# A Perceiver megakernel on one core: a smaller first piece of the context, the first local keys ahead of the query projection, and a new order table

## The chip, the cores and the metric

The kernel runs on one core of a Trainium2 chip. The metric is the device time in microseconds (us) of one execution. TensorE is called PE, its weight loads PEld, VectorE DVE, ScalarE ACT, GpSimd POOL and SyncE SP. Everything is float32; a float32 matmul shows in the trace as two records, so "x4" in a row of the trace is two matmuls.

## The reference, cut to what matters

Two layers of three residual stages each work on 16 batches of 32 tokens with 128 features; the context has 512 rows for each batch. Each stage adds to x what it computes from a layer norm of x.

```python
x = x + L0_xattn(layernorm(x), ctx)   # queries Wq, keys Wk; query i sees keys 16i..16i+15 only ("local")
x = x + L0_attn(layernorm(x))         # RWKV: a scan over the tokens
x = x + L0_ffn(layernorm(x))          # 8 experts, the top 2 of them, and a shared one
x = x + L1_xattn(layernorm(x), ctx, ctx, mask)   # all 512 keys, a mask, softmax
x = x + L1_attn(layernorm(x))         # linear attention and a feed-forward part
x = x + L1_ffn(layernorm(x))          # 16 experts, top 1, a capacity of 32 tokens
```

The keys and values of `L1_xattn` depend on the context alone, so they can be computed at any time after the context is there.

## The kernel before, in words

All 512 tokens fit into one tile of 128 x 512, and so do the 512 keys of one batch. The context stands in SBUF as `ctx`, transposed, 512 columns for each batch. It is loaded by SP in five pieces, given by `PIECES` (line 281): batches 0-1, 2-3, 4-7, 8-11, 12-15. `context(c)` (line 334) issues piece c with its own semaphore `ctx_in{c}`, and `piece_of(b)` says which of them batch b waits for. SP issues, in this order: x, `early` (the first weights), pieces 0, 1, 2, `next`, the first half of the context with tokens in rows (`ctok`), piece 3, `late` (all other weights), piece 4, the second half of `ctok`, and then, behind waits, masks and the weights of the last stage.

The batches go through the middle of the network in two halves (h = 0 and 1) of eight. The work is cut into streams, one generator each, and each `yield` ends a turn:

- `local()` (letter L) is `L0_xattn`. On PE: seven matmuls on zeros (line 1277) from the start on; four transposes of the normalised x (line 1227, called from `turn_lnT`), which wait for DVE's normalised tokens (line 690); the projection of the queries (line 1283), which waits for ACT's copy of those transposes to SBUF (line 487); then for each batch c one matmul with `wk0`, the local keys (line 1306), into bank 0 or 1 in turn. DVE scales the queries (line 722) and multiplies each batch's keys with them (line 732, `prod`); key c + 2 waits for product c, because both use one bank. Then come head sums (line 1294), a softmax, its transposes (line 1315), `z` = probabilities times context (line 1328, with copies by ACT at line 517) and the output (line 1337).
- `projections()` (P) are the keys (line 1266) and values (line 1270) of `L1_xattn`, written to banks 3 and 4 in turn; ACT (lines 498, 500) or DVE (773, 775) copies each out.
- `small_stages(h)` (a, b) are `L0_attn` and `L0_ffn` of half h. On ACT the first of it is exp(w) (line 528), which waits for `late`; DVE's line 784 waits for that. The hidden layer's last product is at line 1411; its silu is at ACT's lines 570 and 571, with a load of the activation table ahead.
- `scores()` (S, line 1438), `exponentials()` (S on ACT, 583), `least()` (S on DVE, 964), `turns()` (T, transposes of the probabilities, line 1452, with copies out of the bank by ACT, 594, or DVE, 975) and `outputs()` (V, 1469) are `L1_xattn`.
- `linear_stages(h)` (c, d) is `L1_attn` and the gate of `L1_ffn`; its transposes are at lines 1558 and 1227, its hidden layer at 1571 and 1584, the counts of the experts at 1609 and 1613, the dispatch at 1626.
- e, h, i, y, o are the last stage: 1643, 1653, 1665, 1677.
- G on PE is `keep_busy` (line 1694): each turn one 128 x 128 matmul into a bank that nothing reads. It puts something on PE where it would wait.

What sets the order on each engine is the table `TURNS` (line 68). It is written out: "L P L8" is a turn of L, a turn of P, eight turns of L. `run` (line 311) goes through it; a letter whose stream is at its end does nothing. Each engine runs its instructions strictly in this order, and waits on semaphores where the data aren't there.

Of the kernel before, what the change touches and what calls it, by code (L numbers as in the profile page):

```python
# [11 lines left out]
P = 128  # L12
BATCH, SEQ, D = 16, 32, 128
TOK = BATCH * SEQ
TT = TOK // P
KEYS = 512
# [5 lines left out]
HB, HT, HTOK = BATCH // 2, TT // 2, TOK // 2  # L22
# [30 lines left out]
def columns(pack):  # L53

    at, out = 0, {}
    for name, n in pack:
# [10 lines left out]

TURNS = {
# [7 lines left out]
    "DVE": (  # L76
# [7 lines left out]
    "ACT": (  # L84
# [4 lines left out]
    "POOL": (  # L89
        "L a L a4 b a3 b L a3 b2 a b4 a b a b3 L c3 d c d L a c d2 a c L b2 d c L c b2 d3 a c b d2 c ")}  # L90

# [26 lines left out]
def program(nc, x_d, early_d, next_d, late_d, ctx_d, ctok_d, mask_d, w1_d, w2_d, moeb_d, out_d):  # L118
    with ExitStack() as stack:
# [5 lines left out]
        def sig(name):  # L125
            if name not in sems:
                sems[name] = stack.enter_context(nc.semaphore(name))
            return sems[name]
# [15 lines left out]
        ctx = sb("ctx", CTX)  # L144
# [133 lines left out]
        mr = [small[:, 64 * i:64 * (i + 1)] for i in range(8)]  # L278
        m4 = [small[:, 516 + 4 * i:520 + 4 * i] for i in range(9)]

        PIECES = (0, 2, 4, 8, 12, BATCH)

        def piece_of(b):

            return sum(1 for p in PIECES[1:-1] if b >= p)

# [44 lines left out]
        def _(sp):  # L331
            def context(c):
                k = slice(KEYS * PIECES[c], KEYS * PIECES[c + 1])
                sp.dma_start(ctx[:, k], ctx_d[:, k]).then_inc(sig(f"ctx_in{c}"), 16)
# [3 lines left out]
            context(0)  # L338
            context(1)
            context(2)  # L340
            sp.dma_start(following[:, :], next_d).then_inc(sig("next_in"), 16)
            sp.dma_start(ctok[0], ctok_d[:, 0:CTX // 2]).then_inc(sig("ctok_in0"), 16)
            context(3)
            sp.dma_start(late[:, :], late_d).then_inc(sig("late_in"), 16)
            context(4)
            sp.dma_start(ctok[1], ctok_d[:, CTX // 2:CTX]).then_inc(sig("ctok_in1"), 16)

            sp.wait_ge(sig("z_ps"), HB)
# [869 lines left out]
        def _(pe):  # L1218
# [24 lines left out]
            def wait_norm(h):  # L1243
                pe.wait_ge(sig(f"lnT_ready{h}"), turned[h])
# [29 lines left out]
            def local():  # L1274
# [4 lines left out]
                pe.wait_ge(sig("early_in"), 16)  # L1279
                turn_lnT(0, X[0], range(TT))  # L1280
                yield
                wait_norm(0)
                mm(Y[0][:, :], wt("wq0"), lnT[:, :], start=True, stop=True).then_inc(sig("q0_ps"), 1)
                yield
                for h in range(2):
# [11 lines left out]
                            last.then_inc(sig("s0_ps"), 1)  # L1297

                    for c in range(HB * h, HB * (h + 1)):
                        if c in PIECES:  # L1300
                            pe.wait_ge(sig(f"ctx_in{piece_of(c)}"), 16)
                        if c % HB >= 2:
                            pe.wait_ge(sig("prod_ready"), c - 1)
                        elif h:
                            pe.wait_ge(sig("z_out"), HB)
                        mm(bank[c % 2][:, :], wt("wk0"), ctx[:, KEYS * c:KEYS * (c + 1)], start=True, stop=True).then_inc(sig("k0_ps"), 1)  # L1306
                        yield
                        if c % 4 == 3 and c % HB > 4:
                            for k in range(c - 7, c + 1):
                                headsum(k)  # L1310
                                if k % 4 == 3:
                                    yield
# [486 lines left out]
```

## Time and profile before

| | us |
|---|---|
| median of 3 runs | 236.79 |
| lowest, highest | 235.16, 237.21 |
| the profiled execution | 235.32 |
| its span, first to last instruction | 233.4 |
| PE busy / DVE / ACT / POOL | 218.7 / 178.0 / 131.7 / 34.5 |
| mean granted clock of PE | 0.993 |

The profiled execution's own time is 1.9 us over its span, and 1.5 us below the median. The share of busy time is a mean over stages with different limits. PE counts as busy from the start of a matmul to its modelled end, so a busy PE isn't PE at its peak. The chain of waits goes back from the last instruction, at each step to what released it. A landing time is counted from the issue of the transfer to its semaphore.

### The profile page before, as it was taken

The numbers are of one execution on the slowest core, as the hardware profiler recorded it, in microseconds if no ns is written. First come the engines' busy times: TensorE is split into PE (matmuls) and PEld (weight loads), VectorE is DVE, ScalarE is ACT, GpSimd is POOL, SyncE is SP. The second block draws the span as 40 slices with busy tenths as digits, with TensorE's granted clock in tenths as the row PEclk, the third lists the DMA queues.
The fourth block names the chain that finished last, engine by engine and source line by source line (L and its number), as shares of the span: only waits on it lengthen the run. The fifth ranks groups of instructions, "written<-read, shape, count | busy, mean of one in ns | idle before, by whom it ended". The sixth has DMA issues, their size and how long they took to land.

```text
span 233.4 us, 5227 instructions
## 1 busy us (share of the span) xinstructions
PE 218.7 (94%) x1992; PEld 156.2 (67%) x1992; DVE 178.0 (76%) x514; ACT 131.7 (56%) x292; POOL 34.5 (15%) x55
## 2 busy tenths in 40 slices
PE   7699999999999999879989998999999989898995
PEld 6332595747786796546656776768577768797495
DVE  2176743999955669999788979999998958646672
ACT  2201473445368327689999987988887741030330
POOL 2120000022205123602040230020001031201000
PEclk9999999999999889999999999999999999999999
DMA  6999959700000000006100340000005998500001
GB/s 204 412 421 448 420 219 213 150 0 0 1 3 0 0 3 0 1 3 159 24 0 0 95 91 3 3 0 4 0 3 177 449 442 386 219 0 0 3 3 45
DMA packets 2905, 26.88 MB, mean 115 GB/s; under 512 B 448, under 2 KB 704, under 8 KB 1344
## 3 DMA queue, kind: packets, MB, share of 16 engines
q1 hardware_dynamic: 2880, 26.54, 31.3%
q8 instruction: 16, 0.26, 0.4%
q14 instruction: 9, 0.07, 0.1%
HBM read 26.28 MB, written 0.26 MB: 114 GB/s over the span
## 4 chain that ended last, share of the span: by engine, by line
PE 72%; DVE 15%; ACT 6%; issue 3%; DMA 3%; SPq 0%; POOL 0%; DVEq 0%
PE bank L1452 8%; PE bank L1328 6%; PE bank L1306 6%; PE bank L1438 6%; PE bank L1266 5%; PE bank L1469 4%; DVE ctx_sb L964 4%; PE bank L1270 3%; DMA ctx_sb<-ctx 3%; PE bank L1411 2%; PE bank L1694 2%; ACT ctx_sb L583 2%; PE bank L1249 2%; PE bank L1394 2%; PE bank L1584 2%
## 5 line engine op out<-in xcount | busy, mean ns | idle before, releaser
L583 ACT ACTIVATE ctx_sb<-ctx_sb,small_sb 128x512 f32<-128x512 f32 x64 | 45.8, 720 | 3.1 <-DVE small_sb L964 3.1
L964 DVE CUSTOM_DVE_ANT_0 ctx_sb<-bank,mask_sb 128x512 f32<-128x512 f32 x64 | 42.2, 683 | 1.7 <-PE bank L1438 1.5
L1452 PE MATMUL bank<-early_sb,ctx_sb 128*128 128x128 f32 x256 | 36.3, 278 | 3.1 <-DVE work_sb L975 2.7
L1452 PEld LDWEIGHTS bank<-early_sb,ctx_sb 128*128 128x128 f32 x256 | 27.9, 141 | 14.6 <-issue 7.9
L385 POOL TENSOR_TENSOR rstd_sb<-veps_sb,minus_half_sb 128x2 f32<-128x2 f32 (+1 forms) x15 | 11.0, 733 | 128.8 <-DVE veps_sb L684 128.8
L594 ACT COPY work_sb<-bank 128x512 f32<-128x512 f32 x40 | 22.9, 579 | 7.7 <-PE bank L1452 7.0
L1438 PE MATMUL bank<-k_sb,work_sb 32*128 32x512 f32 x128 | 18.5, 638 | 1.7 <-DVE small_sb L964 1.1
L1266 PE MATMUL bank<-ctx_sb,early_sb 128*128 128x512 f32 x32 | 16.3, 610 | 1.8 <-DMA ctx_sb<-ctx 1.8
L732 DVE SCALAR_TENSOR_TENSOR work_sb<-bank,early_sb,work_sb 128x512 f32<-128x512 f32 x16 | 11.8, 747 | 8.2 <-PE bank L1306 7.7
L1469 PE MATMUL bank<-work_sb,v_sb 128*32 128x128 f32 x512 | 17.3, 276 | 0.4 <-ACT work_sb L594 0.4
L1270 PEld LDWEIGHTS bank<-late_sb,ctx_sb 128*128 128x128 f32 x128 | 15.4, 191 | 2.8 <-issue 2.6
L1469 PEld LDWEIGHTS bank<-work_sb,v_sb 128*32 128x32 f32 x512 | 13.1, 109 | 5.7 <-ACT work_sb L594 3.5
L975 DVE COPY work_sb<-bank 128x512 f32<-128x512 f32 x24 | 16.4, 682 | 0.5 <-PE bank L1452 0.2
L1270 PE MATMUL bank<-late_sb,ctx_sb 128*128 128x128 f32 x128 | 16.2, 277 | 0.0
L1306 PE MATMUL bank<-ctx_sb,early_sb 128*128 128x512 f32 x32 | 15.8, 605 | 0.2 <-DVE work_sb L732 0.2
L498 ACT ACTIVATE k_sb<-bank,early_sb 128x512 f32<-128x512 f32 x12 | 8.0, 686 | 12.9 <-PE bank L1266 12.9
L517 ACT COPY work_sb<-bank 128x512 f32<-128x512 f32 x16 | 9.2, 583 | 8.3 <-PE bank L1328 8.2
L583 ACT ACTIVATION_READ_ACCUMULATOR ctx_sb<-ctx_sb,small_sb 128x1 f32 x64 | 12.4, 193 | 0.0
L325 DVE TENSOR_TENSOR work_sb<-bank,early_sb 128x512 f32<-128x512 f32 x16 | 10.2, 676 | 0.9 <-PE bank L1315 0.7
L500 ACT COPY v_sb<-bank 128x512 f32<-128x512 f32 x12 | 7.0, 582 | 5.0 <-PE bank L1270 5.0
L1306 PEld LDWEIGHTS bank<-ctx_sb,early_sb 128*128 128x128 f32 x32 | 5.2, 189 | 6.6 <-issue 3.2
L487 ACT ACTIVATE lnT_sb<-bank 128x256 f32<-128x256 f32 (+1 forms) x7 | 2.9, 415 | 11.8 <-PE bank L1227 7.7
(262 smaller groups left out, 403.4 us busy)
## 6 DMA issues: line engine op xcount, KB each, us to landing
k_sb<-moe_w SPq DMA_DIRECT2D x1, 4096.0 KB, 12.8
ctx_sb<-moe_w SPq DMA_DIRECT2D x1, 4096.0 KB, 17.2
ctx_sb<-ctx SPq DMA_DIRECT2D x3, 1024.0 KB, 15.4
late_sb<-late SPq DMA_DIRECT2D x1, 2966.5 KB, 21.7
mask_sb<-ctx_tok SPq DMA_DIRECT2D x1, 2048.0 KB, 14.3
v_sb<-ctx_tok SPq DMA_DIRECT2D x1, 2048.0 KB, 27.8
mask_sb<-mask SPq DMA_DIRECT2D x4, 512.0 KB, 7.9
mask_sb<-mask SPq DMA_DIRECT2D x8, 256.0 KB, 4.5
```

What stands on the lines that cost most here:

```text
L583: s.activation(sc[u % NSC], sc[u % NSC], ACT.Exp, bias=smin[:, u:u + 1], scale=-1.0, accum_out=rsum[:, u:u + 1]).then_inc(sig("p1_ready"), 1)
L594: s.copy(pt[j % NPT], bank[TB[j % 2]][:, :]).then_inc(sig("pT_act"), 1)
L732: v.scalar_tensor_tensor(prod[c % HB].rearrange("p (q j) -> p q j", j=LOCAL), bank[c % 2][:, :].rearrange("p (q j) -> p q j", j=LOCAL), wt ...
L964: v.tensor_tensor_reduce(sc[u % NSC], bank[SB[u % GROUPS]][:, :], mask[:, KEYS * b:KEYS * (b + 1)], MASK_BIG, 3e38, ALU.add, ALU.min, smin ...
L975: v.tensor_copy(pt[j % NPT], bank[TB[j % 2]][:, :]).then_inc(sig("pT_dve"), 1)
L1266: last = mm(dst[:, :], wt("wk1"), ctx[:, KEYS * b:KEYS * (b + 1)], start=True, stop=True)
L1270: last = mm(dst[:, P * k:P * (k + 1)], ctx[:, at:at + P], wt("wv1"), start=True, stop=True)
L1306: mm(bank[c % 2][:, :], wt("wk0"), ctx[:, KEYS * c:KEYS * (c + 1)], start=True, stop=True).then_inc(sig("k0_ps"), 1)
L1328: last = mm(bank[c % 2][:, P * k:P * (k + 1)], ctok[h][:, at:at + P], mix[c % NE][:, P * k:P * (k + 1)], start=True, stop=True)
L1438: mm(bank[SB[g]][:, :], qc[b][r, :], k1[r, KEYS * b:KEYS * (b + 1)], start=True, stop=True)\
L1452: last = nc.tensor.transpose(bank[TB[u % 2]][:, P * k:P * (k + 1)], sc[u % NSC][:, P * k:P * (k + 1)], wt("ident"))
L1469: last = mm((bank[OB2][r, 0:P] if b == BATCH - 1 else bank[OB1][r, at:at + P]), vkey[:, b, k, r], pt[(GROUPS * b + g) % NPT][:, P * k:P * ...
```

## The change

`PIECES` gets a further cut: batch 0 is now a piece of its own (256 KB) and batch 1 another, so the context comes in six pieces, and SP issues one more transfer ahead of the rest. On PE the local keys of batch 0 stand ahead of the projection of the queries. And all four rows of `TURNS` are new. Nothing is computed in another way, and no matmul is added or removed but for `keep_busy`: 32 turns of it are reached before, 24 now.

```diff
-        PIECES = (0, 2, 4, 8, 12, BATCH)
+        PIECES = (0, 1, 2, 4, 8, 12, BATCH)
...
             context(2)
+            context(3)
             sp.dma_start(following[:, :], next_d).then_inc(sig("next_in"), 16)
             sp.dma_start(ctok[0], ctok_d[:, 0:CTX // 2]).then_inc(sig("ctok_in0"), 16)
-            context(3)
+            context(4)
             sp.dma_start(late[:, :], late_d).then_inc(sig("late_in"), 16)
-            context(4)
+            context(5)
             sp.dma_start(ctok[1], ctok_d[:, CTX // 2:CTX]).then_inc(sig("ctok_in1"), 16)
...
                 turn_lnT(0, X[0], range(TT))
                 yield
+                def keys(c):
+                    mm(bank[c % 2][:, :], wt("wk0"), ctx[:, KEYS * c:KEYS * (c + 1)], start=True, stop=True).then_inc(sig("k0_ps"), 1)
+                pe.wait_ge(sig("ctx_in0"), 16)
+                keys(0)
+                yield
                 wait_norm(0)
                 mm(Y[0][:, :], wt("wq0"), lnT[:, :], start=True, stop=True).then_inc(sig("q0_ps"), 1)
...
                     for c in range(HB * h, HB * (h + 1)):
-                        if c in PIECES:
-                            pe.wait_ge(sig(f"ctx_in{piece_of(c)}"), 16)
-                        if c % HB >= 2:
-                            pe.wait_ge(sig("prod_ready"), c - 1)
-                        elif h:
-                            pe.wait_ge(sig("z_out"), HB)
-                        mm(bank[c % 2][:, :], wt("wk0"), ctx[:, KEYS * c:KEYS * (c + 1)], start=True, stop=True).then_inc(sig("k0_ps"), 1)
-                        yield
+                        if c:
+                            if c in PIECES:
+                                pe.wait_ge(sig(f"ctx_in{piece_of(c)}"), 16)
+                            if c % HB >= 2:
+                                pe.wait_ge(sig("prod_ready"), c - 1)
+                            elif h:
+                                pe.wait_ge(sig("z_out"), HB)
+                            keys(c)
+                            yield
...
     "PE": (
-        "L P L P L11 P4 L P L8 P L2 a L2 P L a P L a3 P L P L4 P6 a P L P2 L3 a L2 a2 L P L P L a L a P a2 b "
+        "L P L3 P L9 P4 L P L8 P L2 a L P L2 a P L a3 L P L2 P L2 P6 L P a P L P L3 a L a2 L2 P L a L a L P L "
```

Lines of the new file are 1 to 2 higher than before's up to line 1277, the local keys are at line 1287 in place of 1306, and lines from 1294 on are 10 or 11 higher. The order of the instructions is shown at three places.

**PE, the first matmuls.** Before:

```order
L1277 MATMUL bank<-work_sb 128x256 x7
L1266 MATMUL bank<-ctx_sb,early_sb 128x512
L1227 MATMUL bank<-early_sb,xn_tok_sb 128x128 x4
L1266 MATMUL bank<-ctx_sb,early_sb 128x512
L1283 MATMUL bank<-lnT_sb,early_sb 128x512
L1306 MATMUL bank<-ctx_sb,early_sb 128x512 x8
```

Now:

```order
L1279 MATMUL bank<-work_sb 128x256 x7
L1268 MATMUL bank<-ctx_sb,early_sb 128x512
L1229 MATMUL bank<-early_sb,xn_tok_sb 128x128 x4
L1287 MATMUL bank<-ctx_sb,early_sb 128x512
L1293 MATMUL bank<-lnT_sb,early_sb 128x512
L1268 MATMUL bank<-ctx_sb,early_sb 128x512
L1287 MATMUL bank<-ctx_sb,early_sb 128x512 x7
```

The local keys of batch 0 have taken the place of the second key projection, which now stands behind the queries' projection. Behind these rows PE's order is unchanged up to the start of the second half's local keys. On ACT the copy of the first projection (line 498, now 500) now stands ahead of the copy of the transposed x (487, now 489).

**PE, the linear attention of the second half, some 35 us before the end.** The names: `mask_sb` holds that stage's tiles, `small_sb` the gate's; line 1694 (now 1705) is `keep_busy`. Before:

```order
L1552 MATMUL bank5<-mask_sb 32x128 x8
L1694 MATMUL bank2<-early_sb 128x128 x3
L1558 MATMUL bank5<-early_sb,mask_sb 128x128 x2
L1694 MATMUL bank2<-early_sb 128x128 x3
L1249 MATMUL bank1<-late_sb,mask_sb 128x128 x2
L1694 MATMUL bank2<-early_sb 128x128 x9
L1227 MATMUL bank5<-early_sb,xn_tok_sb 128x128 x2
L1694 MATMUL bank2<-early_sb 128x128 x2
L1609 MATMUL bank7<-small_sb,late_sb 128x32
L1613 MATMUL bank7<-small_sb,late_sb 128x16
L1571 MATMUL bank6<-lnT_sb,late_sb 128x256 x2
```

Now:

```order
L1563 MATMUL bank5<-mask_sb 32x128 x8
L1569 MATMUL bank5<-early_sb,mask_sb 128x128 x2
L1251 MATMUL bank1<-late_sb,mask_sb 128x128 x2
L1620 MATMUL bank7<-small_sb,late_sb 128x32
L1624 MATMUL bank7<-small_sb,late_sb 128x16
L1705 MATMUL bank2<-early_sb 128x128 x7
L1229 MATMUL bank5<-early_sb,xn_tok_sb 128x128 x2
L1705 MATMUL bank2<-early_sb 128x128 x2
L1582 MATMUL bank6<-lnT_sb,late_sb 128x256 x2
```

Six of `keep_busy` around line 1558 and two of the nine behind it are gone, and the counts of the experts (1609, 1613) have moved from behind the transposes to ahead of the keep-busy work. Further on, the seven of `keep_busy` ahead of the last dispatch (line 1626) are four now, and four stand earlier in place of one.

**ACT, the hidden layer of the second half's experts (line 570 is the silu), at some 120 us.** Before:

```order
L556 ACTIVATE mask_sb<-bank,late_sb 128x256
L594 COPY work_sb<-bank 128x512
L556 ACTIVATE mask_sb<-bank,late_sb 128x256
L570 ACT_TABLE_LOAD
L570 ACTIVATE mask_sb<-mask_sb 128x1024
L571 ACTIVATE mask_sb<-mask_sb 64x256
L583 ACT_TABLE_LOAD
```

Now:

```order
L558 ACTIVATE mask_sb<-bank,late_sb 128x256 x2
L572 ACT_TABLE_LOAD
L572 ACTIVATE mask_sb<-mask_sb 128x1024
L573 ACTIVATE mask_sb<-mask_sb 64x256
L596 COPY work_sb<-bank 128x512
L585 ACT_TABLE_LOAD
```

A copy that empties one of the two banks of the transposed probabilities (line 594, now 596) has moved from ahead of the silu to behind it. In that middle part (the second half's small stages beside `L1_xattn`) many turns of S, T and V have changed places by one or two on all engines.

## Rows read from the trace of the kernel before

**Rows 1.** The chain of waits, first 11 us: start us, us, what.

```profile
1.64 6.57 DMA ctx_sb<-ctx
8.25 1.12 PE bank L1266 x2
9.38 0.44 PE bank L1227 x4
9.82 0.86 PE bank L1266 x2
10.68 1.04 PE bank L1283 x2
```

**Rows 2.** Instructions in order of time, first 13 us: start us, us, engine, line, what.

```profile
1.31 5.13 PE L1277 MATMUL bank<-work_sb 128*128 128x256 f32 x14 [1.31 <-POOL work_sb L374]
6.22 1.12 DVE L690 TENSOR_SCALAR xn_tok_sb<-x_tok_sb,aggr_sb,rstd_sb 128x128 f32<-128x128 f32 x4 [1.20 <-POOL rstd_sb L385]
9.94 0.60 ACT L487 ACTIVATE lnT_sb<-bank 128x512 f32<-128x512 f32 x1 [7.71 <-PE bank L1227]
10.43 1.26 ACT L498 ACTIVATE k_sb<-bank,early_sb 128x512 f32<-128x512 f32 x2
11.83 0.75 DVE L722 TENSOR_SCALAR work_sb<-bank,early_sb 128x512 f32<-128x512 f32 x1 [4.49 <-PE bank L1283]
```

**Rows 3.** DMA issues: tile, queue, count, KB each, median us from issue to landing.

```profile
ctx_sb<-ctx SPq DMA_DIRECT2D x2, 512.0 KB, 7.0
late_sb<-late SPq DMA_DIRECT2D x1, 2966.5 KB, 21.7
early_sb<-early SPq DMA_DIRECT2D x1, 294.0 KB, 3.0
```

**Rows 4.** SP's issues in order of time: start us, us for issuing.

```profile
1.17 0.42 SPq L337 DMA_DIRECT2D early_sb<-early  x1
5.67 0.67 SPq L344 DMA_DIRECT2D late_sb<-late  x1
```

**Rows 5.** A stretch while ctx lands: each engine's busy us, PE's clock, DMA share, GB/s.

```profile
6.00:7.00 1.00, 0.44 (x3) 0.04 (x1) 0.78 (x4) 0.00 (x0) 0.43 (x7) 1.00 1.06 365
```

**Rows 6.** In order of time: the third copy of z.

```profile
30.15 0.58 ACT L517 COPY work_sb<-bank 128x512 f32<-128x512 f32 x1 [0.35 <-PE bank L1328]
```

**Rows 7.** Stretches by stage: us, busy us (count) of PE, PEld, DVE, ACT, POOL; clock.

```profile
60.00:92.00 32.00, 31.95 (x220) 25.85 (x218) 23.05 (x70) 17.83 (x35) 7.39 (x7) 0.95 0.00 1
92.00:130.00 38.00, 33.61 (x329) 22.47 (x330) 34.88 (x106) 33.86 (x78) 9.38 (x9) 1.00 0.12 29
```

**Rows 8.** The same columns, a single microsecond inside the first of these stretches.

```profile
81.00:82.00 1.00, 1.00 (x6) 1.00 (x6) 0.78 (x3) 0.00 (x0) 0.29 (x1) 0.50 0.00 0
```

**Rows 9.** Chain of waits: lines 1411 (80 us), 1584, and keep-busy (L1694) in the tail.

```profile
80.27 3.60 PE bank L1411 x16
196.98 0.86 PE bank L1694 x6
202.95 0.45 PE bank L1694 x4
206.38 1.79 PE bank L1584 x16
214.13 1.64 PE bank L1694 x14
```

**Rows 10.** What the tail's keep-busy stands beside, in order of time.

```profile
197.11 0.42 DVE L1069 TENSOR_TENSOR mask_sb<-bank,mask_sb 128x256 f32<-128x256 f32 x1
202.99 0.56 ACT L487 ACTIVATE lnT_sb<-bank,late_sb 128x256 f32<-128x256 f32 x1 [7.36 <-PE bank L1227]
214.96 1.00 DVE L1145 TENSOR_SCALAR v_sb<-late_sb,small_sb 128x512 f32<-128x512 f32 x2
```

**Rows 11.** ACT around the silu of the second half, in order of time.

```profile
121.95 1.28 ACT L570 ACT_TABLE_LOAD   x1
123.25 1.06 ACT L570 ACTIVATE mask_sb<-mask_sb 128x1024 f32<-128x1024 f32 x1
```

More of the change, by code:

```diff
@@ L69 @@
     "PE": (
[6 rows of a table removed]
-    "DVE": (
[7 rows of a table removed]
-    "ACT": (
[4 rows of a table removed]
[6 rows of a table added]
+    "DVE": (
[7 rows of a table added]
+    "ACT": (
[5 rows of a table added]
     "POOL": (
-        "L a L a4 b a3 b L a3 b2 a b4 a b a b3 L c3 d c d L a c d2 a c L b2 d c L c b2 d3 a c b d2 c ")}
+        "L2 a6 b a2 b a4 b10 c L2 c2 b a2 d c d c d b d b L d c d a d L b a c d b d c2 a d L a d c L b c ")}
 class Shifted:
```

33 rows, old and new, of the table TURNS are left out of this document.

## The prediction, made before the changed kernel ran

> **What bounds the kernel now.** I went from the busy time by stage to the chain of waits, and from there to the order of time at the three places that the change touches. By stage: from 60 to 92 us PE is busy for 31.95 of 32 us, and from 92 to 130 us DVE for 34.88 of 38, with PE at 33.61 [rows 7]. So the middle is a queue of work on PE first and on DVE next; whatever starts it earlier moves it as a whole, and changing places within it gains little. The chain shows what starts it. It begins with a transfer: the context's first piece, issued at 1.64 us, lands 6.57 us later, at 8.21, and the first key projection starts at 8.25 [rows 1]. PE's matmuls on zeros ended at 1.31 + 5.13 = 6.44, so PE stands still for 1.8 us. The four transposes stand behind that projection and start at 9.38, though DVE had their input ready at 6.22 + 1.12 = 7.34 [rows 1, 2]. In the tail the chain goes through keep-busy matmuls: 0.86, 0.45 and 1.64 us of it are line 1694, work that nothing reads, but that PE had to finish before the instruction behind it [rows 9].
>
> **The smaller first piece.** It is 256 KB in place of 512. Ahead of it go x, 128 x 512 floats or 256 KB, and `early`, 294 KB [rows 3]. So 806 KB must have come in place of 1062. The trace has no piece of this size in this place; I bound its landing from both sides. The early bound: `early` landed at 1.17 + 3.0 = 4.2 us with 550 KB [rows 3, 4], the old piece at 8.21 with 1062, and a straight line between them gives 806 KB at 6.2; PE is free only at 6.44. The late bound: the last 256 KB cost only their bytes at the 365 GB/s that the engines moved just then [rows 5], which is 0.7 us, so 7.5. No gain at all is possible too, if what the old piece waited for wasn't its own bytes (a rival below). I take the middle of the two bounds, 6.9 us, 1.3 us earlier; none of the two rows is nearer.
>
> Followed from 6.94: projection 1.12 us, transposes 0.44, local keys of batch 0 0.86, as the second projection, of the same shape [rows 1], so PE comes to the queries' projection at 9.36. Its input is ACT's copy, now behind the copy of the projection. That starts at about 8.1, takes 1.26 / 2 = 0.63 [rows 2], and the copy of the transposes 0.60 [rows 2], so it is ready at about 9.35: no wait. The queries' projection then ends at 9.36 + 1.04 = 10.4 in place of 11.7 [rows 1]; DVE's scaling follows 0.1 later as before (11.83, 0.75 us long [rows 2]), and 0.1 behind that the first product, at 11.4 in place of 12.7. The second local keys now stand behind the second projection, and end at 10.4 + 0.86 + 0.86 = 12.1. A product takes as long as the scaling, so the first ends then too, and the second starts at 12.2 in place of 13.4. From there the loop of keys and products is the old one. **Head: 1.2 us gained**, between 0.6 and 1.7.
>
> Taken alone, the swap of keys and projection is worth nothing: the local keys were ready 0.1 us before the first product could start, and are now ready 2 us before. Its cover is the queries' scaling. The extra transfer costs SP some 0.42 us [rows 4] ahead of all later issues. The queue is full then (DMA share 1.06 [rows 5]), so I cost it at nothing. Were the cover gone, `late` would land at 5.67 + 21.7 + 0.42 = 27.8 us. Its first user is ACT's exp(w), now behind the third copy of z, which ended at 30.7 and will end at about 29.5 [rows 3, 4, 6], so the landing isn't waited for.
>
> *A rule against the trace.* The Trainium skill, "DMA: Bandwidth & Descriptors", section "Anatomy of one DMA", gives a transfer a fixed 2.0 us and then its bytes at 436 GB/s. With the bytes queued ahead this would land the new piece at about 4.6 us, and the sum below would be 2.1 in place of 1.65, since only the matmuls on zeros are then left to wait for. By the same rule the old piece would have landed at 5.2, where the trace has 8.21, so I stay with the bounds from the rows.
>
> **The tail.** (a) Three keep-busy matmuls ahead of line 1558 end at 197.84, while DVE's att (line 1069), which 1558 needs, is done at 197.53 [rows 9, 10]. Without them 1558 starts 0.27 earlier. On DVE three gate operations of 0.2 us have moved ahead of the copy behind 1558, which gives back about as much: 0.1 of gain in all. (b) The counts of the experts, 0.35 us, no longer stand between the transposes and line 1571. Two keep-busy matmuls do, to 202.95 + 0.45 = 203.4, and ACT's copy ends at 203.55 [rows 9, 10], so 1571 starts at 203.6 and not 203.75: 0.15. (c) Seven keep-busy matmuls, 1.64 us, end at 215.77; the slots that line 1626 needs first are ready at 214.96 + 0.50 = 215.46, the second ones at 215.96 [rows 9, 10]. With four matmuls (0.95 us) PE waits for those instead: 0.2. **Tail: 0.45 gained**, between 0.1 and 0.8.
>
> **The middle.** By its order PE has the same work between 20 and 92 us, and was never short of it; DVE has the same work from 92 on. I take 0. The bounds: PE stood idle for 4.4 us of the stretch from 92 to 130 and DVE for 3.1 [rows 7]; I allow a better order half of the latter, 1.5 gained. The loss is the rival on ACT's copy.
>
> **The sum.** 1.2 + 0.45 = 1.65. Against its own time the profiled execution would go from 235.32 to 233.7, its span from 233.4 to 231.75. It is 1.5 us below the median of the runs shown. I set the sum against the median: 236.79 - 1.65 = **235.1 us**, 0.7% faster, within the 1% (2.4 us) that a measurement of this kernel can tell from no change.
>
> **The rivals.**
>
> *The clock.* At 81 us the granted clock is 0.50, that is 1.2 in place of 2.4 GHz [rows 8], and the mean of the stretch is 0.95 [rows 7]. Line 1411's 16 records take 3.60 us there, the 16 of line 1584, of the same shape, 1.79 at full clock [rows 9]: 1.8 us lost. Ahead of the fall PE ran matmuls with only 8 rows of weights (lines 1394, 1402). The new order puts a full key projection between them. If the clock then stays up, the time is 235.1 - 1.8 = 233.3. If it falls once more somewhere, as where the eight keep-busy matmuls went, it is 236.9. The Trainium skill, "TensorE: Matmul & The Clock Gate", section "What's actually happening", has the gate look at activity in a window that runs free of the kernel's start, so the same kernel can lose more or less from run to run. By that rule the order alone doesn't decide; the runs, 2 us apart, would fit. Chances: 0.2 for the gain, 0.1 for the loss.
>
> *The piece doesn't land earlier.* For it: 8.21 is late for 1062 KB, which at 365 GB/s [rows 5] take 2.9 us; the transfers behind run beside the first ones, and may hold it up whatever its size. Then the change doesn't do what it says, the head gives 0, and the time is 236.3. Against it: `early`, small and in front, landed after 3.0 us [rows 3]. Chance 0.13.
>
> *Slower: ACT's copy behind the silu.* The copy of one bank of transposes now waits for the table load and the silu, 1.28 + 1.06 = 2.3 us [rows 11]. The bank's next transposes can't start before, and behind them stand the scores for DVE. If PE gets there that early, up to 2.3 us are lost: 235.1 + 2.3 = 237.4. It decides once the stall is over 1.65 us. Against it: between the two uses of the bank the new order has two groups with a wait of their own, some 3 us. Chance 0.13.
>
> The forecast itself keeps 0.44.
>
> **How the numbers follow.** Faster by over 1% is below 234.4: the clock's gain (0.2), and a third of the forecast, where the middle gains or the piece lands at 6.4 (0.14): 0.34. Slower by over 1% is above 239.2: the ACT stall with a second fall of the clock, or several waits in the middle: 0.08. The rest, 0.58, is the same. The range goes from the clock's case with some of the middle's gain, 232.7, to the ACT case with a little more, 237.8; the forecast's own is 234.0 to 236.2.
>
> **What would show it.** In the profile after: the first projection at 6.9 us and not 8.25, and the first product on DVE at 11.4; the start of z at 26.0 in place of 27.15; line 1558 following 1552 at once, 1626's second group starting with its slots. The granted clock at 80 us shows the clock's case, a wait of the transposes for ACT's copy near 123 us the slower one. The forecast is wrong if z starts 1.2 us earlier and the first scores (92.4 us) don't, or if the stretch from 92 to 175 us changes its length by over 1.5.

## The result

The change didn't make the kernel faster. Over 20 executions each it has a median of 235.31 us (234.56 to 238.11), and before, run beside it, 235.30 (232.34 to 237.80). The ratio of change to before is 1.0074, 95% interval 1.0039 to 1.0109, but it leaves out every execution over 1.5% above the fastest of its own kernel, nine of before's and one of the change's; the means of all twenty are 235.43 us before and 236.00 with the change. I had forecast 0.7% faster. What moved is the best case: before reached 232.34 us, the change never less than 234.56.

The chain of waits of the changed kernel, its first 12 us (start us, us, what), answers to [rows 1]:

```profile
1.31 4.69 PE bank L1279 x14
6.00 0.86 PE bank L1268 x2
6.85 0.65 PE bank L1229 x4
7.51 0.86 PE bank L1287 x2
8.37 0.96 PE bank L1293 x2
9.33 0.86 PE bank L1268 x2
```

The transfer is gone from the chain. The first projection starts as the warm-up ends, at 6.00 instead of 8.25. The DMA issues, for [rows 3]:

```profile
late_sb<-late SPq DMA_DIRECT2D x1, 2966.5 KB, 20.4
...
ctx_sb<-ctx SPq DMA_DIRECT2D x2, 256.0 KB, 3.8
ctx_sb<-ctx SPq DMA_DIRECT2D x1, 512.0 KB, 6.1
```

The first product on DVE starts at 10.23 us (12.69 before), z at 24.70 (27.15), the first scores at 88.62 (92.40): 3.8 us are won by there, 2.4 of them by the first projection and most of the rest because PE's clock didn't fall at 80 us in this trace. At the end of the second half's combination (line 1422, once 1411) all of it is gone: 131.02 after, 130.78 before. Stretches of the changed kernel (us, busy us of PE, PEld, DVE, ACT, POOL, then PE's clock, DMA share, GB/s):

```profile
110.00:123.60 13.60, 12.27 (x131) 7.85 (x124) 10.89 (x39) 13.48 (x27) 2.91 (x1) 1.00 0.00 1
123.70:130.40 6.70, 6.70 (x29) 5.92 (x29) 3.64 (x12) 5.70 (x16) 0.00 (x0) 0.50 0.02 4
130.50:198.70 68.20, 65.17 (x810) 47.30 (x808) 60.89 (x187) 48.67 (x119) 8.32 (x11) 1.00 0.36 139
198.80:205.50 6.70, 6.18 (x28) 5.78 (x29) 4.23 (x19) 0.09 (x1) 1.39 (x2) 0.50 0.49 205
```

PE's clock is at 1.2 GHz (0.50 in the rows) twice for some 6.8 us. Before it was so once, for 3.4 us at 80 us [rows 8]. The second fall comes where the keep-busy matmuls were taken away; the first comes in the middle, where none ever stood. PE in the tail of the changed kernel, with its waits in brackets:

```profile
197.31 0.64 PE L1563 MATMUL bank<-mask_sb 128*32 128x128 f32 x16
198.69 0.68 PE L1569 MATMUL bank<-early_sb,mask_sb 128*128 128x128 f32 x2 [0.74 <-DVE mask_sb L1071]
199.88 1.22 PE L1251 MATMUL bank<-late_sb,mask_sb 128*128 128x128 f32 x4 [0.52 <-DVE mask_sb L1076]
```

Where line 1694 had filled these two waits, PE now stands still.

### The profile page after: what moved, and what is told of

It reads as the page before. It is cut to its first block, busy times and chain, and to the rows that moved or that the text cites. A ratio compares the mean times of both kernels' runs of the same rounds, so it can differ in the third digit from the quotient of the medians.

```text
span 235.9 us, 5196 instructions
## 1 busy us (share of the span) xinstructions
PE 222.3 (94%) x1976; PEld 158.0 (67%) x1976; DVE 178.0 (75%) x514; ACT 131.8 (56%) x292; POOL 33.9 (14%) x55
## 4 chain that ended last, share of the span: by engine, by line
PE 74%; DVE 14%; ACT 7%; issue 4%; POOL 0%; DVEq 0%; POOLq 0%
PE bank L1463 11%; PE bank L1339 6%; PE bank L1449 6%; PE bank L1287 5%; PE bank L1480 4%; PE bank L1268 4%; ACT ctx_sb L585 3%; PE bank L1422 2%; DVE ctx_sb L966 2%; PE bank L1251 2%; PE bank L1705 2%; PE bank L1279 2%; PE bank L1272 2%; PE bank L1405 2%; PE bank L1582 2%
## 5 line engine op out<-in xcount | busy, mean ns | idle before, releaser
L1463 PE MATMUL bank<-early_sb,ctx_sb 128*128 128x128 f32 x256 | 38.0, 283 | 2.4 <-DVE work_sb L977 1.1
L1463 PEld LDWEIGHTS bank<-early_sb,ctx_sb 128*128 128x128 f32 x256 | 28.6, 143 | 16.6 <-ACT ctx_sb L585 8.5
L1339 PEld LDWEIGHTS bank<-work_sb,v_sb 128*128 128x128 f32 x64 | 7.9, 192 | 1.5 <-issue 1.3
```

The lines of the kernel that those rows point to most:

```text
L1339: last = mm(bank[c % 2][:, P * k:P * (k + 1)], ctok[h][:, at:at + P], mix[c % NE][:, P * k:P * (k + 1)], start=True, stop=True)
L1463: last = nc.tensor.transpose(bank[TB[u % 2]][:, P * k:P * (k + 1)], sc[u % NSC][:, P * k:P * (k + 1)], wt("ident"))
```

## The experiments

Each execution comes with its mean granted clock, so kernels can be compared at equal clock. Before was run 121 times beside the experiments: 35 executions at 1.000 (.999 counted in) with a median of 232.86 us, 36 at .993 (some 234.5), 19 at .985 (236.3), 28 at .978 (237.1), 3 at .971 (240.0). A step of .007 costs about 1.5 us. "At full clock" below is the median of a kernel's executions at 1.000 or .999, with their number. The kernels were run in five groups, each beside its own executions of before, whose median at full clock went from 232.79 to 233.53 us from group to group (single ones from 231.82 to 233.93); so a difference of under 0.7 us between kernels of two groups is not shown. And since the warm-up (the matmuls on zeros) ends sooner or later in each execution, at 5.8 to 7.4 us in the traces with 14 of its records, the traces are compared from the first projection on (by the line's first record; in the chain it may stand 0.2 us later). S are the scores (line 1449), T their transposes (1463), all us:

```
us from the first projection to    first S  first T  last S  end     first projection at
before (fall at 80 us)              84.1     87.6    168.1   225.2     8.3
e5_first_keys                       82.6     86.0    166.5   223.6     6.2
e1_head                             82.9     87.0    167.5   224.6     6.4
e17_head_pool_back                  82.8     86.2    168.3   225.5     6.8  (fall at 126 us)
e3_tail_back                        82.8     88.4    168.2   225.4     7.3
e11_change_busy32                   82.8     88.4    168.2   225.5     6.5
e8_change_again (tail fall)         82.8     88.4    168.2   226.9     6.8
the change (two falls)              82.8     88.4    171.3   230.0     5.8
```

**The change in halves.** Only rows of `TURNS` are mixed, at points where both orders have done the same turns on an engine.

```diff
 e1_head:      first piece and keys as changed; TURNS of the change up to the first S, of before behind it
 e2_rest:      the inverse
 e3_tail_back: the change, with before's TURNS of the last stage
 e4_mid_back:  the change, with before's TURNS from the first S to the last T
```

> The kernel before with the change's split first piece, its first keys and its order of the first batch stage (up to the first scores of the second), and the old order behind that; all 32 keep-busy matmuls are back. Theory A (the loss lies behind the first stage: a stretch of half clock in the tail, where eight keep-busy matmuls went, and one at 124 us): z starts 2.0 to 2.5 us earlier than before, first scores (92.4 before) as much earlier, ratio to before 0.990 to 0.993. Theory B (the gain of the head is used up by waits wherever the old order was made for later landings): z earlier, time within 0.3% of before. Theory C (the split piece itself costs later, by later transfers): ratio over 1.003.

Ratio 1.0032 (0.998 to 1.008); at full clock 233.1 us (6 of 12), 0.2 over before. The head's 2 us are seen at z (25.3), but only part of them lasts: theory B was nearest.

> The changed kernel with only the last stage's order on the four engines as it was before: 32 keep-busy matmuls, in their old places. Theory A1 (the removed keep-busy matmuls cost the clock at 198 us): no half clock between 190 and 215 us, 2 to 3 us faster than the changed kernel, ratio to before 0.996 or less. Theory A2 (the loss lies in the middle's order, which a dip at 124 us or waits show): ratio to before stays at 1.005 to 1.008.

1.0025 (0.9986 to 1.0064); 10 of 12 executions at full clock, 234.0 us. No fall between 110 us and the end:

```profile
110.00:196.00 86.00, 82.23 (x972) 59.30 (x972) 75.10 (x238) 69.33 (x164) 11.23 (x12) 1.00 0.29 106
196.00:206.00 10.00, 8.94 (x74) 8.07 (x67) 6.50 (x27) 2.24 (x5) 1.39 (x2) 1.00 0.46 189
```

A1 on the clock, though not on the time (A1 had 0.996 or less). Against e1_head, of the same group, the scores' order costs 0.9 us at full clock; in the traces 0.7 up to the last scores and 0.8 to the end. One place of it can be named: the new order has the second turn of scores ahead of the first transposes, and PE waits 1.36 us for DVE there, so the first T comes 1.4 us later than in e1_head.

> The changed kernel with only the scores' and projections' stage (from the first local scores to the last) in its order of before; the tail has 24 keep-busy matmuls as in the change. Theory A1 (the tail costs): ratio to before 1.000 to 1.004, half clock near 198 us remains. Theory A2 (the middle costs): no half clock near 124 us, ratio to before 0.99 to 0.995.

1.0012 (0.9976 to 1.0047), none of 12 at full clock, seven at .993 or .992 with 233.4. In its trace the clock is at half from 126.8 to 130.2 us and from 198.5 to 205.3. The tail's fall stays with the tail's order, A1; that the middle's would go with the middle's order was wrong.

> The kernel before (old pieces, old order of the first stage) with the change's order of the scores' stage and of the tail. Theory A (head gains 2 us, the rest loses 3 to 4): ratio to before 1.012 to 1.017. Theory B (the rest's order was made for an earlier head and loses only in step with it): ratio 1.005 to 1.010. If the head gives nothing that lasts: 1.007, the same as the whole change.

1.0123 (1.0063 to 1.0183), none of 6 at full clock: theory A. Its one trace has a fall of 6.8 us at 79 us and, unlike the change's, none in the tail, though the same 24 keep-busy matmuls stand there and PE has the same two waits of 0.74 and 0.52 us:

```profile
196.00:208.00 12.00, 9.32 (x86) 7.59 (x86) 9.01 (x36) 1.91 (x5) 1.39 (x2) 1.00 0.58 248
```

**The head in parts.**

```diff
 e5_first_keys:  changed pieces and keys; of the change's TURNS only PE's first 6, ACT's and POOL's first 3
 e6_piece_alone: before, with
-        PIECES = (0, 2, 4, 8, 12, BATCH)
+        PIECES = (0, 1, 2, 4, 8, 12, BATCH)
 e7_fewer_busy:  before, with the change's 24 keep_busy turns in the change's places
 e8_change_again: the change
```

> The changed kernel's split first piece and its first keys ahead of the queries' projection, with every other order (the rest of the first stage too) as before. In e1_head the routed combination of the first batch ran with two key projections and the output projection between its halves (72.99 to 78.86, 5.9 us, where before had 75.19 to 80.19, 5.0 us). Theory A (that reordering eats the head's gain): first scores 2 us earlier than before's full-clock time of 90.7 (92.4 less what the half clock cost), at 88.5; at full clock throughout the time is 231.2 to 231.9, against 232.9 of before and 233.1 of e1_head. Theory B (any order but a fitting one waits; the gain is lost between 92 and 175): 232.6 or more at full clock.

At full clock 231.41 us (4 of 12), 1.45 under before: theory A. The ratio is 0.9962 (0.990 to 1.002), since the other eight lose clock as before's do.

> The kernel before with only the first 512 KB of the context sent as two pieces of 256 KB, no turn moved. If the split alone brings the head's gain: first projection at the end of the warm-up (6.0 to 7.4), z 1 to 2.4 us earlier, as in e5_first_keys; if the first keys' place matters, z lies 0.3 us or more behind e5's after the same first projection. At full clock 231.2 to 232.0 by theory A, 232.6 or more by theory B.

231.6 us at full clock (2 of 12), ratio 0.996 (0.990 to 1.002). Within 0.2 us of e5, and z starts 18.8 us behind the first projection in this trace (25.71) and 18.9 in e5's (25.05): the split is the whole gain, the keys' place is worth nothing that shows. But seven of the 12 were at .978, so over all executions little is left: their mean is 234.92 us, before's beside them 235.11.

> The kernel before with the change's 24 keep-busy matmuls in the change's places, instead of 32; nothing else is touched. Theory A (taking the 15 keep-busy matmuls around 197 to 202 us away is what lets the clock fall in the tail): half clock at 197 to 206 us in most executions, none of them at a mean clock of 1.0, time 0.5 to 1.5 us over before at a mean clock lower by .007 or .014. Theory B (the clock's fall in the tail has to do with the other moves): same clocks and time as before, ten of 29 at 1.0.

1.011 (1.0005 to 1.0215), none at full clock, at .985 to .964 (one of six took 1173 us and is left out). Its trace:

```profile
190.00:199.00 9.00, 7.58 (x78) 6.36 (x77) 7.14 (x27) 1.59 (x4) 2.76 (x4) 1.00 0.95 410
199.80:209.50 9.70, 6.63 (x29) 6.26 (x30) 4.17 (x18) 0.57 (x1) 1.39 (x2) 0.50 0.28 117
```

Nothing but these matmuls differs from before, and the clock is at half for 10 us: theory A. The same trace has a fall of 3.4 us at 128 us, so the fall in the middle comes with before's order of it too.

> The changed kernel itself beside the others on this chip. Theory A: no execution at a mean clock of 1.0, ratio to before 1.003 to 1.010; half clock in the tail (198 us) again where the trace is taken, with or without one at 124 us.

1.0131 (1.005 to 1.021), none of 6 at full clock; its trace has the tail's fall and not the one at 124 us. As expected.

**Combination, keep-busy, warm-up.**

```diff
 e9_split_combination: e5, PE's turns 70 to 80 as changed
 e10_busy_early: e5, with 2 + 3 + 3 keep-busy matmuls into bank 0 around line 1405
 e11_change_busy32: the change, keep_busy 32 times and where before had it
 e12_short_warm: e5, with
-                for _ in range(7):
+                for _ in range(5):
```

> e5_first_keys with the change's order of TensorE alone between the second batch's last sums over the context tokens and the routed combination (the output projection and a key projection between the combination's two halves). At a mean clock of 1.0 e5 had 231.4, e1_head, with all of the first stage's new order, 233.2. Theory A (this split is the price of the new order): combination's first to the base's first matmul 3.5 instead of 2.6 us, 232.2 to 232.6 at full clock. Theory B (the price lies in the order of VectorE and ScalarE or earlier on TensorE): 231.3 to 231.7. And if the denser TensorE there holds the clock at 75 to 85 us, fewer executions at 0.978 than e5's 4 of 12.

1.0132 (1.008 to 1.018), none of 6 at full clock. PE's rows:

```profile
75.70 1.13 PE L1405 MATMUL bank<-work_sb,late_sb 8*128 8x256 f32 x4
77.00 0.68 PE L1251 MATMUL bank<-following_sb,o_sb 128*128 128x128 f32 x4 [0.18 <-ACT o_sb L523]
77.52 1.02 PE L1268 MATMUL bank<-ctx_sb,early_sb 128*128 128x512 f32 x2
78.48 1.13 PE L1405 MATMUL bank<-work_sb,late_sb 8*128 8x256 f32 x4
80.05 0.71 PE L1413 MATMUL bank<-late_sb,work_sb 8*128 8x128 f32 x4 [0.45 <-DVE big_sb L937]
```

From 1405 to 1413 it takes 4.3 us, 2.6 in e5 and 3.5 in e1_head: PE's order without DVE's and ACT's costs more than the three together. The clock still fell at 82 us (and at 130). Neither theory had the size.

> e5_first_keys with eight keep-busy matmuls (two, three and three, into a PSUM bank that nobody reads then) around the first batch's routed combination at 73 to 78 us, where its slower executions lose clock. Theory A (thin work there lets the clock fall): full clock behind it in most executions, none at 0.978, median 231.9 to 232.6 against e5's 233.95; the eight cost 0 to 0.9 us by themselves. Theory B (the fall comes whatever stands there): clocks as e5's, every level 0.3 to 0.9 us later.

1.0096 (1.0035 to 1.0156), none of 6 at full clock. From 1405 to 1413 it takes 4.3 us as well, 1.7 more than in e5, and the clock fell at 80.0 all the same. Theory B, but at more than its price. The price was too low: seven of these matmuls take 1.64 us [rows 9], so eight take about 1.9 (an estimate), and the chain here was delayed by nearly all of it.

> The changed kernel with before's 32 keep-busy matmuls in before's places of the tail, every other turn as in the change. Theory A (the tail's other moves are worth nothing, the keep-busy matmuls hold the clock): as e3_tail_back, 233.6 to 234.2 at full clock, half or more of the executions there. The gain of 0.45 us that the prediction gave the tail's moves would show as 233.4 or less at full clock. Theory B (the tail's clock falls by the moves, not by the matmuls taken away): none at full clock, 235 or more.

1.0006 (0.9957 to 1.0055), 3 of 6 at full clock, 234.3 us. With the 32 matmuls back the changed tail can keep the clock, and its other moves gain nothing against e3_tail_back (234.0).

> e5_first_keys with 10 warm-up matmuls instead of 14 ahead of the first projection. If the first projection waits for the warm-up and not for its piece: it starts 0.5 to 1 us before e5's 6.2, and shows when the piece has landed (5.4 by its 3.8 us from an issue at 1.64). Theory A (the head's gain is bounded by the warm-up): 0.3 to 1 us faster at the same clock if the clock has risen, slower by up to 1 us if the clock rises only after the first projections. Theory B (the piece bounds it): the same start, and the same time.

0.9938 (0.988 to 0.999), an interval under 1. The chain:

```profile
1.65 4.29 DMA ctx_sb<-ctx
5.99 1.13 PE bank L1268 x2
7.11 0.58 PE bank L1229 x4
```

Now the transfer is in the chain again: the 256 KB land at 5.94. With seven warm-up matmuls (14 records) the first projection started at 5.8 to 7.4 in the traces, by when the clock rose. At full clock 231.54 us (1 of 6), no better than e5; at .993 233.2, where e5 has 233.9.

**What the first stage's order costs, and the keep-busy matmuls' places.** In e13 and e14 the first stage's new order is split in two; e15 moves keep-busy matmuls.

```diff
 e13_combination_all: e5, turns around the routed combination as changed on PE, DVE and ACT
 e14_all_but_combination: e5, all the rest of the first stage as changed
 e15_busy_moved: the change; of its 24 keep_busy the 8 ahead of the last dispatch go to 197-203 us
 e16_piece_short_warm: e6 and range(5) for the warm-up
```

> e5_first_keys with the change's order of the stretch around the first batch's routed combination (some 70 to 80 us) on TensorE, VectorE and ScalarE together; e9 moved TensorE alone there. Theory A (the price of 1.7 us lies here, and e9's further 2 us came from VectorE's order, which did not fit): combination to base 3.5 us as in e1_head, 232.5 to 233.2 at full clock (e5 231.4, e1_head 233.2). Theory B (it lies earlier): 231.2 to 231.8.

> e5_first_keys with all the rest of the change's order of the first stage, and before's order around the routed combination. Theory A: 231.2 to 231.8 at full clock, combination to base 2.6 us. Theory B: 232.5 or more. Both parts at half the price (0.8 each) would give 232.2 here and in e13.

e13: 231.5 at full clock (3 of 12), ratio 0.9960 (0.9915 to 1.0005). e14: 232.95 (6 of 12), and its trace 0.9 us behind e5's from the first T on. Its ratio is 0.9943 (0.990 to 0.998), but over all 12 executions nothing is left of that: five were at .978 or .977 with some 238.1 us, and the mean is 235.26 beside before's 235.14. My theory A fell: the price is not in the combination.

> The changed kernel with its 24 keep-busy matmuls, but the first 17 of them in before's places, around the idle time at 197 to 203 us, and the eight ahead of the last combination (215 us) left out. Theory A (the place at 197 to 203 us counts, not the number): some executions at a mean clock of 1.0, where the change had none of 26, at 233.6 to 234.4 there. Theory B (the number counts): none at 1.0.

1.0065 (1.003 to 1.010), none of 12 at full clock, nine at .993 with 236.0. The tail of its trace:

```profile
196.00:206.00 10.00, 9.17 (x73) 8.06 (x66) 6.51 (x27) 2.24 (x5) 1.39 (x2) 1.00 0.44 183
...
215.70:218.90 3.20, 3.20 (x11) 1.85 (x13) 0.42 (x1) 0.37 (x1) 0.00 (x0) 0.54 0.00 0
```

and PE ahead of the fall:

```profile
212.79 0.41 PE L1620 MATMUL bank<-small_sb,late_sb 128*128 128x32 f32 x2 [1.14 <-DVE small_sb L1128]
213.04 0.39 PE L1622 MATMUL bank<-small_sb,late_sb 128*128 128x32 f32 x2
214.94 3.48 PE L1637 MATMUL bank<-v_sb,xn_tok_sb 128*128 128x256 f32 x8 [1.52 <-DVE v_sb L1147]
```

The fall has moved from 198 us to 215, where the eight now lack. Theory B's forecast came true, but its reason, the number, doesn't explain that the fall moved: it came where the matmuls were missing. It isn't the only way to a fall there: e6 and e13 have one of 3.4 us at 214.6 and 211.8 with all 32 in place. And the place sets the price: from the first projection to the end e15's trace takes 227.1 us, 1.6 over e11's, for 3.4 us at half clock.

> The kernel before with the split first piece and 10 instead of 14 warm-up matmuls, no turn moved. Theory A (head gain only, the piece lands at 6.0): first projection at 6.0, 231.2 to 231.8 at full clock, ratio to before 0.990 to 0.998 over all, a version that beats both kernels. Theory B (the shorter warm-up lets the clock rise late): first projections at half clock, 232 or more.

231.7 at full clock (3 of 12), but a ratio of 0.9987 (0.993 to 1.004), so e12's lead isn't confirmed by its simpler sister. (The mean of its 12 executions is 233.95 us, of before's 35 beside them 235.14.)

**GpSimd's order.** DVE and POOL at 90 us; e5_first_keys:

```profile
88.58 0.91 POOL L435 TENSOR_TENSOR mask_sb<-mask_sb 128x256 f32<-128x256 f32 x1
...
89.42 0.69 DVE L839 TENSOR_TENSOR_SCAN mask_sb<-mask_sb 128x264 f32<-128x264 f32 x1
89.45 1.15 POOL L438 TENSOR_TENSOR mask_sb<-mask_sb 128x256 f32<-128x256 f32 x1
...
90.55 1.50 POOL L413 TENSOR_TENSOR work_sb<-work_sb,late_sb 128x768 f32<-128x768 f32 x1
```

and e14_all_but_combination:

```profile
88.17 2.43 POOL L413 TENSOR_TENSOR work_sb<-work_sb,late_sb 128x256 f32<-128x256 f32 x2 [3.84 <-DVE work_sb L954]
...
89.77 1.39 DVE L839 TENSOR_TENSOR_SCAN mask_sb<-mask_sb 128x264 f32<-128x264 f32 x1
...
90.56 1.12 POOL L435 TENSOR_TENSOR mask_sb<-mask_sb 128x256 f32<-128x256 f32 x1
```

In e14 the wide query product stands ahead of line 435. DVE's scan begins while it runs and ends at 91.16, 0.60 us after the product is over (90.56): about its own 0.69 us, counted from there. In e5 it is POOL's 438 that begins 0.03 us behind the scan and takes 1.15 instead of 0.68. The first scores' scaling (line 966) and so the first T come later by about what the scan lost.

```diff
 e17_head_pool_back: e1_head, POOL's row of TURNS as before behind its first three turns
 e18_pool_alone: e5, POOL's row as changed
```

> e1_head with GpSimd's order alone as before (the wide query product behind the two products of the second batch's recurrence, not ahead of them). Theory A (the scan of VectorE is held up by GpSimd's wide product): the scan at 90 us back to 0.69 us, from the first projection to the first transposed scores 86.0 to 86.3 us instead of 87.0, and 0.5 to 0.8 us off e1_head's 233.2 at full clock, 232.4 to 232.7. Theory B (the scan is held up by something else, or costs nothing on the path): 233.0 or more.

231.97 at full clock (6 of 12), 1.1 under e1_head; scan 0.69, first T after 86.2 instead of 87.0: theory A. Ratio 0.9972 (0.993 to 1.001). None of its 12 executions was under .992 or over 234.62 us; their mean is 233.07, that of before's 23 beside them 235.36.

> e5_first_keys with GpSimd's order alone as in the change, the inverse of e17. Theory A: the scan at 90 us 1.2 to 1.4 us instead of 0.69, 0.5 to 0.8 us over e5's 231.4 at full clock, 231.9 to 232.2. Theory B: 231.3 to 231.6.

The scan took 1.39. The ratio is 1.0059 (1.0015 to 1.0102), 234.34 at full clock (6 of 12), 2.9 over e5, four times the expectation. 1.0 of it is another place of the same row: `edges()` (398) now stands behind the standard deviation (387). DVE waited 1.2 us ahead of its own clearing of a tile (line 789), which stands in DVE's order ahead of what PE waited for:

```profile
59.56 0.29 POOL L398 MEMSET mask_sb<- 128x8 f32 x6
60.04 0.27 DVE L789 MEMSET mask_sb<- 128x256 f32 x1 [1.22 <-PE bank L1339]
...
61.00 2.02 PE L1339 MATMUL bank<-work_sb,v_sb 128*128 128x128 f32 x16 [0.96 <-DVE work_sb L326]
```

The profile infers PE as the releaser of line 789, but in kernel.py it waits for `edges_ready`, which comes from line 398: that ran at 57.54 in e5 and at 59.56 here. From the first projection to the end e18's trace takes 227.0 us, 3.3 over e5's, and it has the fall at 80 us, which costs before 1.5; about 1.8 is left, near the sum of the two prices. The rest of the 2.9 lies ahead of the first projection or between the groups (e18's before was at 233.53 at full clock) and stays open.

## Why the prediction was wrong

**The head: right mechanism, size too small, and one cover missed.** I bounded the landing by 6.2 and 7.5 us and took 6.9; it was 5.94 in e12, and 5.83 or earlier in the change's trace, where the first projection starts then: under both bounds. A straight line through two landings was no lower bound. The prediction's 4.6, by "DMA: Bandwidth & Descriptors" of the Trainium skill, was too early by 1.3 us; the section it used is about transfers that GpSimd issues, and these are SP's. What then holds the first projection is the warm-up, which I had at 6.44 as if it were fixed: it ended at 5.8 to 7.4. The term was 1.2; in medians at full clock it measures 1.45 (e5) and 1.3 (e6). The swap of keys cost and gained nothing, as said (e5 and e6). The rival that the piece doesn't land earlier fell.

**The middle: "By its order PE has the same work ... I take 0" is the first step that failed.** The runs show a loss of some 2.6 us at full clock in its place. The bounds of gain and loss looked at idle time and at one copy. Two pieces of the new order cost, at full clock: the first stage's 1.7 us (e1 against e5), of which 1.1 come back with POOL's row alone (e17; 0.8 of them in the trace, up to the first T), and the scores' order 0.9 (e3 against e1). The 1.7 and the 1.1 compare two groups. Set against its own group's before, e5 is 1.7 us under, e1 0.3 over and e17 1.6 under, so POOL's row may be nearly the whole price. Within one group e14 is 1.5 over e13. A part of the medians' differences may also come from where the warm-up ends in the executions that reach full clock: from the first projection on, the traces of e5 and e1 differ by only 0.9, those of e1 and e3 by 0.8. By the prediction's own sign this step failed as well: from the first to the last scores it takes 88.5 us with the change and 83.9 before, 85.4 where the middle's fall is absent (e8). I hadn't looked at POOL at all: at 14% of the span it seemed free. But the price of its order was paid by DVE. This is the sharing told in the Trainium skill, "SBUF — State Buffer", section "SBUF: two separate sides": one pair of ports is lent whole to a GpSimd operation or to a VectorE operation with two SBUF inputs, and the other waits. The rows of e5 and e14 agree both ways round, with 0.69 us drawn out to 1.39 and 0.68 to 1.15.

**ACT's copy behind the silu** moved as shown, and cost no stall of the transposes. In e3 the copy ran at 122.99 and the transposes started at 124.97 without a wait.

**The tail: "0.45 gained" is the second step that failed; it is a loss.** (a) and (c) took away matmuls that stood in the chain, at no price but their time. No run isolates what (a) and (c) gain by the chain; e11 against e3 shows no gain from the rest. But those matmuls helped to keep the clock. The kernels with 24 of them had 0 of 61 executions at full clock (the change 26, e2 6, e4 12, e7 5, e15 12); with 32, before had 35 of 121, e3 10 of 12, e11 3 of 6, and the others 37 of 114, though e9 and e10 had none of 6 each. e7, which differs from before in nothing else, is the cleanest of these. The matmuls don't decide it alone: of the six traces with 24, five have a fall in the tail and e2's has none, and of the fourteen with 32 two have one (e6, e13). One fall of 6.8 us in the tail cost 1.3 us (e8 against e11, 226.88 against 225.54), the change's other one, in the middle, 3.2 more. This was the loss in my rival on the clock, "as where the eight keep-busy matmuls went", at 236.9 and a chance of 0.1. It should have been the main case: I had seen two waits of half a microsecond filled by them. What brings the fall in the middle stays open. It came with the new scores' order (the change) and with before's (e4, e7, e9, e17), and is missing in e8, the same kernel as the change, whose PE was just as busy ahead of that place.

**The clock at 80 us** stayed up, as that rival's other side had it (0.2). Of the ten traces with before's order at the combination seven fell at 80 us (before, e2, e6, e7, e10, e16, e18; not e5, e12, e14), of the nine with the new order on all engines none did (the change twice, e1, e3, e4, e11, e13, e15, e17). It may be why e3 was at full clock 10 times of 12; the change lost it again in the tail. Since each trace is one execution, this is a strong hint, and no measured gain.

The sum, at full clock and against 232.86: head -1.45, the first stage's order +1.7, the scores' order +0.9, the tail's clock +1.3 gives 235.3; the change had 235.2 at .985, its commonest level (10 of 20). This sets the change's commonest level against before's best one. Before loses clock too, in 86 of 121 executions, and so the medians are alike.

**Luck.** The forecast of 235.1 us lies 0.2 under the measured median, 235.31, and that is luck. It was counted from 236.79, the median of three executions; before's median of twenty was 235.30. From there the same sum gives 233.65.

No version that I ran beats both kernels beyond doubt. e5, e6, e12, e13, e16 and e17 are 0.9 to 1.45 us under before at full clock. The ratios are 0.994 for e12 (6 executions) and e14, and 0.999 for e12's sister e16. By the mean of all executions e17 looks best, 233.07 us beside 235.36, in one group of 12.

## What to carry to other kernels

Before taking away work that nothing reads, ask which wait of TensorE it fills, and look at the granted clock of many executions, not of one: the loss shows as a best case that no longer occurs. Price a changed order on every engine that shares something with the one that bounds, GpSimd with its few instructions too. And where a transfer leaves the critical path, find what stands right behind it before crediting the whole wait: here the warm-up, 0 to 1.4 us later.

## What the runs showed of the hardware

Clock falls don't need an idle engine by the profile: from 119.5 us of the change to the fall at 123.6 PE's rows have no gap, and from 110 us it was busy for 12.27 of 13.60 us. They lasted 3.4, 6.8 or 10.2 us, began at other places in other executions of one kernel (the change: 123.6 and 198.7 us in one trace, 197.4 alone in another), and came behind waits of 0.5 to 1.5 us or matmuls with 8 rows of weights; behind the same two waits of 0.74 and 0.52 us e2's clock stayed up. A 256 KB piece behind 550 KB landed 1.65 + 4.29 = 5.94 us into the span (e12), the 512 KB one at 8.21 (before). And an operation of 0.69 us on VectorE took 1.39 beside a GpSimd product of 1.5 us (e14), with none of the wait shown as idle time: it stands in the duration.
